# Cross-attentions of a gated decoder: stacked 128-row scores, nine steps of a batch over two PSUM banks, 16-bit halves on GpSimd

## The reference

```
x = x + tanh(g_xattn[0]) * xattn0(layernorm(x), ctx, ctx, key_mask)
x = x + tanh(g_ffn[0])   * ffn(layernorm(x))
x = x + tanh(g_xattn[1]) * xattn1(layernorm(x), ctx, ctx, causal_mask, padding_mask)
x = x + tanh(g_ffn[1])   * moe(layernorm(x))

# xattn0 (xattn1: adds causal_mask to scores, replaces scores of padded keys by -1e9)
Q, K, V = (query @ Wq + bq, key @ Wk + bk, value @ Wv + bv)  # 16 heads (H) of 16 channels (DK)
scores = einsum('bhqd,bhkd->bhqk', Q, K) / 4;  masked keys get -inf
out = einsum('bhqk,bhkd->bhqd', softmax(scores), V) @ Wo + bo   # 0 where every key is masked
```

## Time and profile before

| what | value |
|---|---|
| median of three runs | 1421.59 us (1419.83 to 1423.03) |
| the profiled execution | 1424.71 us |
| its span in the trace | 1423.0 us |
| mean granted TensorE clock | 0.95 of 2.4 GHz |
| layer 0: the eight batches, from the first maximum | 63.52 to 240.10 us |
| layer 1: the eight batches, from the first maximum | 762.04 to 955.30 us |

### The profile page before, as it was taken

The page is one execution under the profiler, slowest core; times in us unless marked ns, Lnnn a source line. Parts: engine busy times, 40 slices in busy tenths (PEclk is TensorE's granted clock), DMA queues, the critical chain, the costliest instruction groups (busy, mean ns, idle before and its releaser), DMA issues. The chain is left out here.

```text
span 1423.0 us, 35569 instructions
## 1 busy us (share of the span) xinstructions
PE 1272.8 (89%) x13975; PEld 1001.2 (70%) x13975; DVE 1135.9 (80%) x2068; ACT 903.0 (63%) x2071; POOL 280.4 (20%) x242
## 2 busy tenths in 40 slices
PE   1699998689899989899979999995799999999996
PEld 1477676367767767677745776764589999898995
DVE  5578877679999999999655777767698888888884
ACT  1477776248667677677635676653377777677772
POOL 2000000100000000000000000000246666666663
PEclk9899999889999999999799999996699999999999
DMA  8000000133353353433310000000977887788770
GB/s 234 16 6 9 6 2 2 41 91 77 102 154 77 101 135 77 120 105 91 100 60 17 9 6 6 2 2 10 307 220 229 246 246 230 227 247 246 226 194 25
DMA packets 172067, 152.99 MB, mean 108 GB/s; under 512 B 62589, under 2 KB 154386, under 8 KB 171906
## 3 DMA queue, kind: packets, MB, share of 16 engines
q1 hardware_dynamic: 151906, 129.51, 30.2%
q0 software_dynamic: 13936, 16.79, 6.1%
q10 hardware_dynamic: 6064, 4.46, 1.1%
HBM read 116.89 MB, written 36.70 MB: 108 GB/s over the span
## 5 line engine op out<-in xcount | busy, mean ns | idle before, releaser
L1874 POOL DMA_INDIRECT out<-m_yo,m_xg x70 | 161.4, 2306 | 131.0 <-DVE m_yo L1990 115.4
L1896 ACT ACTIVATE m_hf<-m_ps,m_bue 128x256 f32<-128x256 f32 x280 | 117.3, 471 | 105.7 <-PE m_ps L84 105.7
L1062 ACT ACTIVATE f_pr<-f_ps,f_nb 128x256 f32<-128x256 f32 x256 | 107.9, 477 | 71.2 <-DVE f_nb L1345 70.9
L82 PE MATMUL m_ps<-m_ds,m_hs 128*128 128x256 f16 x560 | 152.6, 273 | 0.3 <-DVE m_yo L1990 0.3
L84 PE MATMUL m_ps<-m_ds,m_hs 128*128 128x256 f16 x560 | 152.6, 273 | 0.0
L83 PE MATMUL m_ps<-m_ds,m_hs 128*128 128x256 f16 x560 | 152.6, 273 | 0.0
L82 PE MATMUL m_ps<-m_xt,m_us 128*128 128x256 f16 x560 | 152.6, 273 | 0.0
L84 PE MATMUL m_ps<-m_xt,m_us 128*128 128x256 f16 x560 | 152.6, 273 | 0.0
L83 PE MATMUL m_ps<-m_xt,m_us 128*128 128x256 f16 x560 | 152.6, 273 | 0.0
L480 ACT ACTIVATE x_pr<-x_ps,x_mx 128x120 f32<-128x120 f32 x512 | 143.3, 375 | 7.5 <-DVE x_mx L695 7.0
L699 DVE SCALAR_TENSOR_TENSOR x_pt<-x_ps,x_pt 120x512 f16<-120x512 f32 x128 | 88.3, 690 | 53.3 <-ACT x_pt L488 52.4
(11 more groups left out here) (373 smaller groups left out, 3863.2 us busy)
## 6 DMA issues: line engine op xcount, KB each, us to landing
m_uraw<-in_L_ffn_Wup SPq DMA_DIRECT2D x35, 1024.0 KB, 5.8
m_draw<-in_L_ffn_Wdown SPq DMA_DIRECT2D x35, 1024.0 KB, 5.7
head_values<-f_v_row SPq DMA_DIRECT2D x16, 520.0 KB, 5.0
f_vh<-head_values SPq DMA_DIRECT2D x16, 520.0 KB, 3.9
head_outputs<-f_at_row SPq DMA_DIRECT2D x16, 512.0 KB, 3.8
f_at_in_t<-head_outputs SPq DMA_DIRECT2D x16, 512.0 KB, 5.4
expert_values<-f_pv_row SPq DMA_DIRECT2D x8, 512.0 KB, 2.8
f_pv_in_t<-expert_values SPq DMA_DIRECT2D x8, 512.0 KB, 5.6
```

The lines of the kernel that those rows point to most:

```text
L82: pe.matmul(out, lhs[0], rhs[0], start=(n == 0), stop=False)
L1062: ins = act.activation(pr[h % 2][:, ti, :], S(h)[:, ti, :], ACT.Exp, bias=nb[h % 2][:, ti:ti + 1])
L1874: pool.indirect_dma_start(rows_of, bass.IndirectOffsetOnAxis(xg[j % RING][:, ti, D:D + 1].bitcast(I32), 0), yo[j % 2][:, ti, :], None, bou ...
L1896: ins = act.activation(hf[:, q, m, :], U(q)[:, m, :], ACT.Gelu, bias=weights.bue[par][:, 2 * q + m:2 * q + m + 1], scale=UNSPLIT)
```

## The change

- **Scores.** Two products of 128 rows and 240 columns replace the mask product and six products of 32 rows. Each pair of heads has a stack of rows: 32 rows high query by high key, 32 high by low, 32 low by high, and 32 for the mask (rows 96 to 127: a constant on the query side, masked keys on the key side). The 24 causal products of a batch in layer 1 stay.
- **Stacks through memory.** SP stores the halves of K and of Q in DRAM and reads them back in the order of the stacks: twelve DMAs for a batch. The masks of all batches come with one load at the start.
- **Halves.** `limbs` makes both halves of K, Q and V from 32 bits, for batch 0 on VectorE and from batch 1 on GpSimd (in layer 1 with a product that clears masked keys).
- **Steps.** `tensor_steps` gives nine steps of a batch (CTX, XN, K, Q, V, and for each half of the queries HO and OUT, the way back) places in the units, with K and what it needs two batches ahead. They take turns over two banks (`BANK_TURN`), with a pair of semaphores for each.
- **Other.** ScalarE makes the normalised x (from a product with 1/deviation and a bias) and copies Q once; nothing is spread. VectorE takes the maxima one unit ahead of its other work. In layer 0 the factor for batches without live keys goes into the normalisation of the output. At a stage's start eight steps run, with 24 idle products between them and 16 behind. The setup loses `head_of`, `odd_of` and `mask_w`.

The diff, cut to its core:

```diff
+TERMS = ((0, 0), (0, 1), (1, 0))
+XA_FIRST = ((CTX_T, 0), (XN_T, 0), (K_T, 0), (Q_T, 0), (CTX_T, 1), (XN_T, 1), (V_, 0), (K_T, 1))
+XA_IDLE = (3, 3, 4, 6, 2, 2, 2, 2)
+XA_IDLE_STACKS = 16
+def tensor_steps(b, u):
+    steps = {0: [(Q_T, b + 1)], 1: [(OUT_T, b - 1, 0)], 2: [(V_, b + 1)], 3: [(CTX_T, b + 2), (HO_T, b - 1, 1)],
+             5: [(XN_T, b + 2), (OUT_T, b - 1, 1)], 7: [(K_T, b + 2), (HO_T, b, 0)]}.get(u, [])
...
+        def limbs(eng, chain, b, kind):
...
+            chain(eng.tensor_copy(high, full))
+            eng.tensor_tensor(low, full, high, ALU.subtract).then_inc(limbs_made, 1)
...
         @block.sync
+            def stack_keys(b):
+                sp.wait_ge(limbs_made, LIMBS * b + LIMBS_K)
+                sp.dma_start(k_d[par].rearrange("l p m k -> p l m k"), ks[par][:]).then_inc(rows_out, 16)
+                if b >= 2:
+                    sp.wait_ge(s_ready, XA_UNITS * (b - 1))
+                sp.dma_start(k_stack[par][MASK_AT:P].rearrange("p a i k -> p (a i) k"),
+                             bcast_mid(mask_rows[MASK_AT:P, b, :], H)).then_inc(k_in, 16)
+                sp.wait_ge(rows_out, 16 * (2 * b + 1))
...
+            def stack_queries(b):
+                sp.wait_ge(limbs_made, LIMBS * b + LIMBS_Q)
+                sp.dma_start(q_d[par].rearrange("l p m q -> p l m q"), qt[par][:]).then_inc(rows_out, 16)
+                sp.wait_ge(rows_out, 16 * (2 * b + 2))
...
             for b in range(B):
+                stack_keys(b)
+                stack_queries(b)
+                if b + 2 < B:
+                    load(b + 2)
...
         @block.gpsimd
+            for b in range(1, B):
+                for kind in (K_T, Q_T, V_):
+                    limbs(pool, chain, b, kind)
...
         @block.tensor
             def score(b, u):
                 if u == 0:
-                    pe.wait_ge(km_ready, b + 1)
-                    pe.wait_ge(mask_ready, b + 1)
+                    pe.wait_ge(k_in, 16 * (2 * STACK + 1) * (b + 1))
+                    pe.wait_ge(q_in, 16 * STACK * (b + 1))
...
-                pe.matmul(S(u), s.mask_w[:, layer, :], bcast_mid(mb[par][:], HG), start=first, stop=False)
                 for m in range(C):
-                    for n, (ql, kl) in enumerate(((0, 0), (0, 1), (1, 0))):
-                        last = pe.matmul(S(u)[:, 2 * m:2 * m + 2, :], qt[par][rows, ql, m, ti * P:ti * P + P],
-                                         km[par][rows, kl, m, :, :], start=False, stop=(m == C - 1 and n == 2))
+                    pair = RG * m + r
+                    last = pe.matmul(S(u)[:, 2 * m:2 * m + 2, :], q_stack[par][:, pair, ti * P:ti * P + P],
+                                     k_stack[par][:, pair, :, :], start=(layer == 0), stop=(layer == 0 or m == C - 1))
...
         @block.vector
+            maxima(0, 0)
             for b in range(B + 1):
                 for u in range(XA_UNITS):
-                    if b < B:
-                        maxima(b, u)
+                    if XA_UNITS * b + u + 1 < XA_UNITS * B:
+                        maxima(b + (u + 1) // XA_UNITS, (u + 1) % XA_UNITS)
                     earlier(b, u, XA_LAG - 1, pt_part)
```

More of the change, by code:

```diff
@@ L368, in xattn_stage @@
         ks = two("ks", [P, 2, C, SK], F16)
-        km = two("km", [P, 2, C, 2, SK], F16)
+        q_stack = two("q_stack", [P, PAIRS, SQ], F16)
+        k_stack = two("k_stack", [P, PAIRS, 2, SK], F16)
+        limb_q, limb_k = sb("limb_q", [P, 1]), sb("limb_k", [P, 1])
+        q_d = [nc.dram_tensor(f"{t}queries{i}", (2, P, C, SQ), F16).ap() for i in range(2)]
+        k_d = [nc.dram_tensor(f"{t}keys{i}", (2, P, C, SK), F16).ap() for i in range(2)]
         vf = two("vf", [SK, D])
         va = two("va", [SK, 2, H, DK + 1], F16)
-        mb = two("mb", [P, SK], BF16)
-        keep = two("keep", [P, SK])
-        live = two("live", [P, 1])
+        if layer == 0:
+            live = sb("live", [P, B])
+        else:
+            keep = sb("keep", [P, B, SK])
+            zeros = sb("zeros", [P, WIDE])
         mx = two("mx", [P, HG])
@@ L445, in _, with normalised_x @@
         @block.scalar
         def _(act):
[L447 to L459, removed]
+            def normalised_x(b, ti):
+                tile = TPB * b + ti
+                act.activation(xn[b % 2][:, ti, :], s.x[:, tile, :], ACT.Identity, bias=nmr[:, tile:tile + 1],
+                               scale=s.rstd[:, tile:tile + 1]).then_inc(xn_ready, 1)
@@ L462, in evacuate @@
                                              bias=s.bqk[:, 4 * layer + 2 + m:4 * layer + 3 + m], scale=UNSPLIT / DK ** 0.5)
[L463 to L472, removed]
+                    ins.then_inc(freed(what)[0], 1)
             def exps(b, u):
@@ L488, in pt_part @@
                 act.activation(pt[u % 2][:, 0], PT(u), ACT.Copy, scale=SPLIT).then_inc(pt_hi, 1)
[L490 to L497, removed]
+            act.wait_ge(nmr_ready, 1)
+            for ti in range(TPB):
+                normalised_x(0, ti)
+            for what in XA_FIRST:
+                if what == (CTX_T, 1):
+                    for ti in range(TPB):
+                        normalised_x(1, ti)
+                if what[0] != V_:
+                    evacuate(what)
             for b in range(B + 1):
@@ L658, in evacuate @@
[L658 to L663 removed]
+            def evacuate(what):
+                kind, b = what[0:2]
+                par, front = b % 2, bank(what)
+                if kind == V_:
+                    dve.wait_ge(*produced(what))
+                    if b >= 2:
+                        dve.wait_ge(limbs_made, LIMBS * (b - 2) + LIMBS_V)
+                    dve.scalar_tensor_tensor(vf[par][:], front[0:SK, 0:D], 1.0 / SPLIT, s.bv[0:SK, layer, :],
+                                             ALU.mult, ALU.add).then_inc(freed(what)[0], 1)
+                    return
+                dve.wait_ge(hi_made, HIGH_TURN[what] + 1)
+                if kind == XN_T:
@@ new lines, in _ @@
+            dve.scalar_tensor_tensor(nmr[:], s.mv[:, :, 0], -1.0, s.rstd[:], ALU.mult, ALU.mult).then_inc(nmr_ready, 1)
+            dve.wait_ge(masks_loaded, 16)
+            if layer == 0:
+                chain(dve.tensor_reduce(live[:], m_all[:], AX_X, ALU.min))
+                chain(dve.tensor_scalar(live[:], live[:], -1.0, 1.0, ALU.mult, ALU.add))
+            else:
+                dve.tensor_scalar(keep[:], m_all[:], -1.0, 1.0, ALU.mult, ALU.add).then_inc(masks_made, 1)
+            for what in XA_FIRST:
+                if what[0] in (CTX_T, XN_T, V_):
+                    evacuate(what)
+                if what[0] in (K_T, Q_T, V_) and what[1] == 0:
+                    limbs(dve, chain, 0, what[0])
```

400 lines of the change are left out of this document (214 added, 186 removed).

## The result

The change takes 1364.01 us in the median of four runs (1360.37 to 1366.41) against 1420.71 of the kernel before on the same chip: 0.9598 of its time (95% interval 0.9569 to 0.9626), 57 us less. The forecast was 1357 us, from 1335 to 1395. The profiled execution of the change has a span of 1363.9 us, 59.1 under that of before.

A forecast was written before the change was run, and what follows sets the result against it. TensorE was taken to bound layer 1's cross-attention and be closest to the limit in layer 0. Batches -32 and -39, starts +7.5, setup -1.2 made -65 us: 1421.59 to 1357 us, range 1335 to 1395.

The forecast's parts named there:

- Terms of -32, -39, +7.5 and -1.2: Predicted changes in us: layer 0's eight batches, layer 1's eight batches, both stage starts together, and the setup.
- Score products: Cross-attention units: mask product (0.30) goes, six products become two at 0.12; TensorE saves 0.78 us a unit, 6.2 a batch.
- the 19.5 forecast for a batch: Layer 1 at 2.4 GHz: TensorE's 18.95 us if it never waits, plus 3% because ScalarE is nearer to it.
- both stay beside the other work: Cross-attention batches: ScalarE (16.2 us in layer 0) and VectorE (15.7) stay hidden; layer 0's limit passes to ScalarE.
- the sign named for it: Profile after, layer 0: batches of 17 to 19 us with ScalarE busy above 85%.
- An eighth of layer 0's work at 1.2 GHz: Slow-clock share in layer 0's batches: 17.6 x 0.88 + 24 x 0.12 = 18.4 us a batch.
- The rival with half of layer 0 slow: Half of layer 0 and a tenth of layer 1 at 1.2 GHz: 1382 us in all; chance 0.18.
- the one that stays at 1.2 GHz: All of layer 0 at 1.2 GHz; 1448 us with half of layer 1's work there too; chance 0.04.
- +3.5 and +4: Stage starts of layers 0 and 1: first score waits for halves through memory; 18.2 against 14.76 us in layer 0.
- an issue takes 0.36: Stage start: each DMA issue on SP priced at 0.36 us, so six key reads take 2.2 and three issues 1.1.
- Costed at nothing: GpSimd's halves (some 5 us of 18 a batch) and the DMAs, hidden, with 2 us to spare for the stack.
- a sign of being wrong: The prediction is wrong if score products wait for DMAs in the middle of a stage.

The follow-up runs named there:

- the run that brings 4.9 of the 6.4 us back: The changed kernel with six more products of 128 rows and 240 columns before each unit's scores, results overwritten: 1398.75 us, 0.9826 of before.
- the maxima in turn: The changed kernel with VectorE taking a unit's maxima in that unit's turn, not one unit ahead: 1397.88 us, 0.9817 of before.
- the halves sooner: The changed kernel with VectorE, not GpSimd, making all halves, key halves in unit 0 and query halves in unit 1: 1378.67 us, 0.9691 of before.
- The run with both edits: The changed kernel with batch 0's query-stack transfers on ScalarE's queue and GpSimd's constant rows written after batch 0's query halves: 1351.34 us, 0.9511 of before.

## Why the prediction was right, and where it was not

**Sum.** Terms of -32, -39, +7.5 and -1.2 stood for what came as -36.6, -44.4, +21.3 and -0.6. The total holds by luck: two errors of opposite sign, 10 us in the batches and 14 in the starts, met.

**Score products.** Priced at 0.12 us each, they cost 0.10. Loads of 128 rows hide, as the earlier trace rows said: six products with six loads follow one another in 0.61 us. Layer 1 did stay with TensorE (18.49 of 19.22; the forecast was 18.95 and 19.5), and the lost products are worth 3.7 us a batch there by the run that brings 4.9 of the 6.4 us back. But that alone would not have done it: the 19.5 forecast for a batch came from TensorE's 18.95 "if TensorE never waits, as now", and with the maxima in turn a batch takes 21.4. The prediction gave the early maxima no term; they are worth 34 us. What the runs took away one at a time (34, 35 and 15 us) need not add up to the whole gain, and no run undid the nine steps over two banks, so that their share is not shown.

**Layer 0's limit.** The step "both stay beside the other work", for ScalarE and VectorE, with ScalarE as the limit, failed. The loads themselves came nearly as forecast (ScalarE 15.87 us for 16.2, VectorE 15.27 for 15.7), and so did the sign named for it, ScalarE busy above 85% (15.87 of 18.19). Yet no engine's work is paid for in full at the full clock: VectorE's at about half (1.3 for 2.5; 0.8 for 1.4, with 1.3 less for ScalarE), ScalarE's at a third (0.4 for 1.3), TensorE's at a quarter (1.1 for 4.9). The batch came out at 18.2 and not 17.6 at the full clock, and the 0.8 that the prediction added for a slow clock in every batch made up for it, by luck: 18.4 forecast.

**The clock.** An eighth of layer 0's work at 1.2 GHz was too much. Its mean was 0.96 (before 0.95), the middle batches ran at 1.00; it fell in the first, in the second (100 to 102 us in the rows above) and in the last. The rival with half of layer 0 slow, and the one that stays at 1.2 GHz, did not come. The runs with the maxima in turn and with the halves sooner show what the term was meant for: there the clock fell in each batch from the fourth on and cost some 0.9 us a batch. Why it held in the change and not there is open.

**The start** was the term that was mis-sized: +3.5 and +4 became +9.1 and +12.2 (the second with the scatter above). The step that failed is "an issue takes 0.36", from a store in the earlier trace rows: a key read takes 0.63 and three query reads 1.87, which makes 2.4 us more for the nine. The kind of transfer is not all of it: the same query store took 0.60 behind SP's six reads and 0.38 on ScalarE's queue. And the prediction priced VectorE's instructions as if GpSimd were not there. The run with both edits accounts for 5.5 and 7.3 us; removing both leaves 3.7 and 4.8 over before, about the forecast.

**Costed at nothing.** GpSimd's six instructions are busy 3.85 us of 18.2 and hidden. The stack was said to have 2 us to spare; it has none, and TensorE waits 0.77 us for it in the middle of layer 0. The prediction had named such a wait as a sign of being wrong; the run with the store on GpSimd shows that it is covered. The short pieces did not land late: a key read of 30 KB lands 2.2 us after its issue, a query read of 128 KB 2.8. What the rule of the Trainium skill (DMA: Bandwidth & Descriptors, Specifications) would have made the slow part was slow in the issue, not in the landing.

## What to carry to other kernels

When several engines take turns in a loop, the busiest is not the whole limit: price an engine's work by moving a known piece onto it and off it, compare batches at the same clock, read in the trace what the moved piece took in its new place, and look for the operation whose early start opens the loop. A way through memory costs issue time in the queue that carries it, so read what stands ahead of a store in that queue, above all at a stage's start, where nothing hides it. A sum that comes out right may hold two errors; check its terms against the stretches.

## What the runs showed of the hardware

Three kinds of VectorE instruction that neither read nor write PSUM, begun while a GpSimd instruction that reads SBUF ran, ended just behind it: a cast of 0.3 us became 1.92, a subtraction of 0.41 became 2.04, a normalisation of 0.40 became 0.99. Instructions that read PSUM kept their times beside the same copies (0.69). The Trainium skill (SBUF — State Buffer, Who interferes with whom) says that the two engines share a pair of ports: where a VectorE cast or `tensor_scalar` uses it, whichever engine came first holds it for a whole instruction, and a VectorE instruction with two SBUF inputs contends with a GpSimd instruction that reads SBUF; the traces agree, for all three. In the middle of a stage of the changed kernel it cost nothing that could be seen: there most of VectorE's instructions read PSUM. The normalisation of 0.99 us stands in the run that moved it to VectorE.
